# A selective-scan layer on one core: beta added by an accumulating DMA, and one more state's product on POOL

## The reference, cut to what matters

```
# selective scan: dt, Bm, Cm and z come from projections of x; 256 channels, 16 states per channel
h[n] = exp(A[n] * dt) * h[n] + dt * B[n] * x          # along time, for each state n
y    = sum over n of h[n] * C[n]  + D * x
y    = (y * silu(z)) @ w_out.T + b_out
pre  = y + residual
out  = (pre - mean) / sqrt(var + eps) * gamma + beta  # norm 3, with gamma and beta
x    = layernorm(residual + out)                      # norm 4: residual + beta + gamma * normed
# then the feed-forward layer starts with its own layernorm (norm 5), and norm 6 ends the model
```

## Time and profile before

| | |
|---|---|
| median of 3 runs | 1092.55 us (1088.25 to 1092.70) |
| the profiled execution's own time | 1091.53 us |
| its span, first to last instruction | 1089.7 us |
| mean granted clock of TensorE | 0.966 of full speed |
| DVE busy | 934.5 us (86% of the span) |
| POOL busy | 716.1 us (66%) |
| ACT busy | 847.9 us (78%) |
| PE busy | 977.5 us (90%), with modelled ends |

### The profile page before, as it was taken

The page is one execution under the profiler, slowest core; times in us unless marked ns, Lnnn a source line. Parts: engine busy times, 40 slices in busy tenths (PEclk is TensorE's granted clock), DMA queues, the critical chain, the costliest instruction groups (busy, mean ns, idle before and its releaser), DMA issues. The chain is left out here.

```text
span 1089.7 us, 17921 instructions
## 1 busy us (share of the span) xinstructions
PE 977.5 (90%) x5598; PEld 738.8 (68%) x5598; DVE 934.5 (86%) x1232; ACT 847.9 (78%) x1650; POOL 716.1 (66%) x603
## 2 busy tenths in 40 slices
PE   6999999999978999998657599999999989997987
PEld 4677777777754555555545487777777777786776
DVE  7999999999963897965799999999999999999851
ACT  7778878878746668767877889898998989897843
POOL 3456466766761111323779999998989989998630
PEclk9999999999998999999778799999999999999899
DMA  6443434433415002112987768477676757776401
GB/s 187 124 143 114 139 110 141 122 94 116 120 52 195 0 1 78 39 39 88 245 167 168 137 155 170 118 179 153 164 147 164 151 135 188 151 151 141 88 4 38
DMA packets 93921, 133.86 MB, mean 123 GB/s; under 512 B 8706, under 2 KB 48642, under 8 KB 93828
## 3 DMA queue, kind: packets, MB, share of 16 engines
q1 hardware_dynamic: 93828, 132.73, 49.1%
HBM read 116.45 MB, written 14.16 MB: 120 GB/s over the span
## 5 line engine op out<-in xcount | busy, mean ns | idle before, releaser
L2345 DVE TENSOR_TENSOR_SCAN oa<-bank_a,h,oa 128x512 f32<-128x512 f32 x128 | 159.7, 1269 | 12.7 <-ACT h L2020 9.8
L2345 DVE TENSOR_TENSOR_SCAN ob<-bank_a,h,ob 128x512 f32<-128x512 f32 x128 | 160.1, 1268 | 10.2 <-ACT bank_a L2011 6.1
L1820 PE MATMUL bank_m<-w,f_h 128*128 128x256 f32 x448 | 104.3, 383 | 0.0
L1491 POOL TENSOR_TENSOR oa<-ob,x1T 128x1024 f32<-128x1024 f32 x8 | 18.8, 2355 | 129.5 <-DVE ob L1391 129.5
L2011 ACT ACTIVATE bank_a<-s,A 128x512 f32<-128x512 f32 x128 | 86.8, 684 | 17.8 <-DVE ob L2345 8.9
L2011 ACT ACTIVATE bank_a<-dtc,A 128x512 f32<-128x512 f32 x128 | 86.9, 684 | 14.1 <-DVE ob L2345 6.9
L1765 PE MATMUL bank_y<-ident,ob 128*128 128x128 f32 x512 | 71.2, 285 | 26.1 <-POOL ob L2581 14.4
L1820 PEld LDWEIGHTS bank_m<-w,f_h 128*128 128x128 f32 x448 | 84.7, 192 | 14.2 <-issue 3.6
L1765 PEld LDWEIGHTS bank_y<-ident,ob 128*128 128x128 f32 x512 | 62.6, 147 | 36.6 <-POOL ob L2581 15.3
L883 POOL TENSOR_TENSOR xd<-xs,L 128x512 f32<-128x512 f32 x32 | 34.0, 1063 | 76.1 <-DVE xs L662 76.1
L1765 PE MATMUL bank_y<-ident,oa 128*128 128x128 f32 x512 | 70.9, 284 | 14.1 <-DVE oa L2351 14.0
(11 more groups left out here) (403 smaller groups left out, 2925.8 us busy)
## 6 DMA issues: line engine op xcount, KB each, us to landing
Bb<-CB_rows SPq DMA_DIRECT2D x128, 256.0 KB, 6.1
Cb<-CB_rows SPq DMA_DIRECT2D x128, 256.0 KB, 5.8
abc<-decays SPq DMA_DIRECT2D x32, 512.0 KB, 4.4
Ebc<-ramps SPq DMA_DIRECT2D x64, 128.0 KB, 3.1
uT<-in_uT SPq DMA_DIRECT2D x8, 512.0 KB, 4.2
u<-in_u SPq DMA_DIRECT2D x8, 512.0 KB, 3.9
x_tokens<-x2s SPq DMA_DIRECT2D x8, 512.0 KB, 3.5
x_rows<-x1T SPq DMA_DIRECT2D x8, 512.0 KB, 2.9
```

The lines of the kernel that those rows point to most:

```text
L1820: i = e.matmul(to, f_h[:, k, c * CH:(c + 1) * CH], w2[:, k, :], start=False, stop=(c % 2 == 1 and k == KF - 1))
L2345: e.tensor_tensor_scan(s[:, k, :], p_a[k][:, :], s[:, k, :], h0[:, n, k:k + 1], ALU.mult, ALU.add).then_inc(v_s, 1)
```

## The change

- `shifted` no longer computes: POOL issues a DMA that reads the row beta from DRAM, 1 KB for each of 4 token groups and each of 128 partitions (512 KB in all), and adds it to `x2` in SBUF. `summed` waits for this DMA instead of for POOL's sum. In the last block (`end_shifted`, L2661) the sum stays on POOL; only its count starts at 0.
- State 3 joins `on_pool`: its product leaves DVE, where it stood between the scans of states 4 and 5, and stands on POOL between `into(cur, 6)` and `into(cur, 7)`. ACT's `spread_C(cur, 3)` goes. All counts that are worked out from `on_pool` follow: SP's `load_C(7)` now waits for POOL's product of state 3, PE's `add_up(3)` too, and `into(7)` too.

```diff
+            beta_row = d["everywhere"].rearrange("(a o n) -> a o n", a=1, o=1)[:, :, sum(n for _, n in EVERYWHERE) - DM:]
-            p_g, on_pool = d_sem("p_g"), (0, 12, 14)
+            p_g, on_pool = d_sem("p_g"), (0, 3, 12, 14)
 # ACT
                         decay(cur, 4, 1)
-                        spread_C(cur, 3)
                         carry(cur, 3)
 # DVE
-                    e.wait_ge(p_xb, Z + p + 1)
+                    e.wait_ge(p_xb, p + 1)
                         scan(cur, 4, 1)
-                        product(cur, 3)
                         scan(cur, 5, 0)
 # POOL
                 def shifted(b):
                     e.wait_ge(v_pre, 2 * b + 2)
-                    e.sem_inc(step, 1)
-                    e.tensor_tensor(x2, x2, rowwise(bet), ALU.add).then_inc(p_xb, 1)
+                    e.dma_start(x2, beta_row.to_broadcast([P, NC, DM]), accum_op=ALU.add).then_inc(ld_beta, DMAS)
                 def summed(b):
                     e.wait_ge(p_gam, b + 1)
-                    e.wait_ge(p_xb, b + 1)
+                    e.wait_ge(ld_beta, DMAS * (b + 1))
                         into(cur, 6)
+                        product(cur, 3)
                         into(cur, 7)
```

More of the change, by code:

```diff
@@ L1563, in build @@
             p_b, p_l3, p_xb, p_gam, p_add, p_l4, p_l6 = (d_sem("p_" + n) for n in ("b", "l3", "xb", "gam", "add", "l4", "l6"))
-            ld_xT, ld_x2, st_o = (d_sem(n) for n in ("ld_xT", "ld_x2", "st_o"))
+            ld_xT, ld_x2, st_o, ld_beta = (d_sem(n) for n in ("ld_xT", "ld_x2", "st_o", "ld_beta"))
             pair, single = (p_m[0], p_m[2]), p_m[1]
```

## The result

The changed kernel takes 1097.55 us, the median of 15 runs (1091.74 to 1099.05); the kernel before took 1091.69 us on the same chip (15 runs, 1088.25 to 1094.96). Over all these runs the ratio of after to before is 1.0043, with a 95% interval of 1.003 to 1.0056: a loss of 4.7 us (3.3 to 6.1), small and clear of no change. The profiled execution took 1096.12 us with a span of 1094.3, against 1091.53 and 1089.7 before.

What follows compares the result with a forecast made beforehand. POOL's turn was to set the period: 2.63 - 2.47 + 1.7 = 1.86 us in each of 7 periods, 13.0 less 6.9 us of waits, +6.1 us on 1091.53, 1097.6, taken as 1098; range 1087 to 1110.

Steps and rivals of the forecast that it cites:

- The issue: POOL's time to issue the accumulating DMA in place of `shifted`: taken as 1.7 us, bounds 0.38 to 4.9 us.
- 7 x (0.16 + X) - 6.9: POOL's added time over 7 periods: product +2.63, sum -2.47, X for the DMA's issue, less 6.9 us of waits.
- the break-even: Issue time on POOL at which its longer turn just uses up its waits for statistics: 0.83 us.
- the 6.9 us of room: POOL's waits for DVE's statistics ahead of `norm45`, 5 places over all blocks, taken off the added time as one sum.
- Rival D: Nothing shows: POOL's issue between 0.8 and 1.6 us, loss under 5.4 us; chance 0.22.
- ACT's gain: ACT's copy of C for state 4 comes 0.35 us earlier each period, at most 2.8 us in 8 blocks.
- rival B: DVE sets the pace: the full 1.11 us comes out in each of 8 blocks, -8.9 us, 1083.6; chance 0.10.
- rival A: Light issue, 0.4 to 0.8 us: POOL keeps its room, ACT's 0.35 us sets the time, 1088 to 1092; chance 0.17.
- "nothing" for `add_up(3)`: PE's `add_up(3)` starts at 796.94, POOL's product is there at 795.4: no cost.
- The new wait: POOL's `summed` waits for the DMA's landing: 17 us of cover from six POOL instructions, against 7.2 for a load; no cost.
- SP's queue: B of state 9, issued behind C of state 7, lands at 801.9, wanted at 802.7: no cost, 0.8 us to spare.
- Rival C: DMA lands over 17 us after issue or delays state 9's B over 0.8 us; landing at 19 gives 1112; chance 0.09.

Runs made afterwards that it cites:

- the first and seventh experiment: Changed kernel with state 3's product back on DVE, DMA kept: 1.0013 of the kernel before; the same with POOL's sum in block 0's tail: 1.0016.

## Why the prediction was right, and where it was off

**The number.** Of the forecast 1098 us the measured median, 1097.55, is only 0.5 us off, and part of that is luck: the sum was +6.1 us and the loss by the ratio is 4.7. The issue was taken 1.9 us too dear in all, and the rest of the sum 0.5 us too cheap. The loss forecast as likeliest was one of over 0.5%; it was 0.43%.

**What sets the time.** POOL's turn does, as forecast: the instructions that POOL has to run one behind the other in a period. The runs, put beside the prediction's formula 7 x (0.16 + X) - 6.9 with X as POOL's timeline of each has it (to the start of the next instruction; without POOL's idle time behind it):

| kernel | X, us | formula | period by period | measured, us (95%) |
|---|---|---|---|---|
| no beta | 0 | none | 0.3 | 0.0 (-1.6 to 1.5) |
| plain DMA | 0.91 | 0.6 | 2.4 | 4.4 (2.7 to 5.9) |
| 4 KB pieces | 1.03 | 1.4 | 2.8 | 3.1 (1.5 to 4.5) |
| the change | 1.43 | 4.2 | 4.4 | 4.7 (3.3 to 6.1) |
| part of the sum, no DMA | 1.57 | 5.2 | 5.3 | 5.4 (3.5 to 7.2) |
| POOL's sum kept | 2.47 | 11.5 | 11.6 | 11.6 (9.5 to 13.7) |
| two DMAs | 2.57 | 12.2 | 12.3 | 12.0 (9.9 to 14.1) |

The measured column is ratio less one, times the median of before on the same chip. The waits of ACT for `norm45` grow roughly with X: 5.1 us without beta, 7.3 with the plain DMA, 7.6 in the changed kernel, 7.3 with part of the sum, 10.2 and 9.6 in the last two. From 1.4 us on the formula holds within 0.5 us. The plain DMA shows that it fails below; the 4 KB pieces lie 1.7 us above it, at the edge of their interval.

**The mis-sized term: the issue.** I took 1.7 us, from the power of 128x8 numbers; the row has 1.35 us and 1.43 to the next start. That is 7 x 0.27 = 1.9 us of my 6.1; the sum with the measured term is +4.2 against the measured +4.7. The Trainium skill (DMA: Bandwidth & Descriptors, Specifications and Anatomy of one DMA) has about 1 µs to the first byte of a DMA through GpSimd, and calls the generation of descriptors small. That isn't the same quantity, but the plain copy's 0.83 us of POOL's own time is near it, and the accumulating one's 1.35 us isn't small where POOL sets the pace.

**The step that was wrong in form: the break-even.** I pooled the 6.9 us of room over seven periods, and so had a break-even at an issue of 0.83 us. But the prediction itself reads that two of the seven have no room, and I now take it that room doesn't pass from one period to the next. Tail by tail, POOL waited in the kernel before 0, 0, 1.6, 1.6, 1.6, 0.8 and 1.2 us. A turn longer by G = 0.16 + X costs G less the period's room, and never less than zero; for the plain DMA that is 2 x 1.07 + 0.27 = 2.4 us, and for the change 2 x 1.59 + 0.79 + 0.39 = 4.4. The column "period by period" is this. It is worked out after the result and no run tests it alone, but the measured times of the two kernels in question lie nearer to it. The plain DMA still costs 2.0 us more than it gives; that is of the size of the 1.4 and 1.7 us that the DMA alone costs in the first and seventh experiment, and the kernel that would tell, the issue's 0.9 us of POOL's time without a DMA, was not run.

This count is not the whole of it either. The sum that went stood ahead of `norm36`, the product that came stands behind it. In the kernel without beta POOL takes 21.68 us from `norm36` to `norm45` (810.78 less 789.10) where it took 20.68 (809.49 less 788.81), although the 1.61 us of wait for the statistics are gone from it. So the product alone uses up the room ahead of `norm45`, whatever beta costs, and an issue can hide only in the wait for norm 3's statistics. The prediction read that wait (1.1 us) and left it out of its sum. In the kernel without beta it is 0, 0, 0.8, 1.4, 0.7, 0 and 0.2 us, tail by tail. Counted from there the plain DMA would cost 3.8 us, which fits, and the change 7.0 us, which is above its interval. Neither count fits every kernel.

One reading of a row was wrong without harm to the sum: the waits for rows of B are not mostly in block 0. Of the 8.4 us, 2.2 lie there and 6.2 in the later blocks; the changed kernel still has 5.2 of these.

Rival D, a small loss with an issue between 0.8 and 1.6 us, is in truth where the change landed: my own mechanism, at its lower end.

**ACT's gain.** The prediction's 0.35 us a period is there: from the scans of state 4 to the copy of C for that state's product it was 3.76 us before and is 3.32 now. By `stats4` 0.28 us of it are left in the changed kernel, and 0.46 us in the one without beta. ACT's timeline of the changed kernel, against the earlier trace rows, has the copy of C right behind the carry, without the 0.35 us of idle time:

```profile
795.37 0.69 ACT L2029 ACTIVATE xc<-bank_m,columns 128x512 f32<-128x512 f32 x1 [0.63 <-PE bank_m L40]
795.96 0.19 ACT L2022 ACTIVATE h<-oa 128x2 f32<-128x2 f32 x1
796.05 0.59 ACT L2018 ACTIVATE bank_c<-Cb 128x512 f32<-128x512 f32 x1
```

The 8.9 us of rival B are refuted by the kernel without beta: no issue holds POOL there, and the time is that of before. The prediction reckoned with up to 2.8 us of rival A in that case; the measured 0.0, with 1.6 us of gain as its bound, shows less. The rows show one place where they went. `norm36` waits for norm 3, which lies ahead of state 4, and from there to the next `drive` POOL has hardly a gap and one instruction more; this stretch is 33.26 us (822.36 less 789.10), and with it the period shrinks by only 0.18 us of the 0.46. No run has the product ahead of `norm36`, so this stays a reading of the rows. Another candidate is the rows of B.

**PE.** I had "nothing" for `add_up(3)`. The rows show 0.51 us: POOL's product ends at 798.46, and PE takes `add_up(3)` up at 799.66, since the matmuls of two other products (the first of them at 796.11) stand ahead of it in its own order.

```profile
793.35 1.98 PE L40 MATMUL bank_m<-s,w_xz 128*128 128x512 f32 x4 [1.43 <-ACT xc L2029]
...
797.93 1.89 PE L1822 MATMUL bank_m<-w,f_h 128*128 128x256 f32 x8
799.66 1.04 PE L1767 MATMUL bank_y<-ident,oa 128*128 128x128 f32 x8
```

From the x projection to `add_up(3)` it is 6.31 us, exactly as in the earlier trace rows. PE's order didn't move, and DVE, early now, reaches it too soon. I looked for a cost at POOL's product; it is in PE's program.

**The new wait and SP's queue.** `summed` never waited in the changed kernel's profile; it comes 18.3 us after the issue's start, and the landings take 9.4 to 12.4. Rival C happened once in the eight profiles with POOL's DMA, with the product on DVE: 18.0 us of landing and 3.0 us of wait in the first tail. "Nothing" for the load of state 9's B was too kind, as a statement on B's rows altogether: they land 1.2 us later in the median in the changed kernel, and 0.4 to 1.6 us later in all the others, with the product on POOL or POOL's DMA or both. I take the product's part, without a run that shows it, for the loads that SP issues in a bunch once POOL's product of state 3 frees their buffer.

**What stays open.** The early blocks: three kernels that left one or both alone gave 1.0032, 1.0032 and 0.9991, none of it clear of the kernel that it is to be compared with. The 1.4 and 1.7 us of the DMA alone, whose intervals begin at 1.0000 and 1.0001. And why the plain DMA, with an issue 0.5 us shorter, costs nearly as much as the change.

## What to carry to other kernels

Where engines are busy for 91 to 96% of a period, taking an instruction off the busiest of them is worth only what the next-late engine allows, here 0.46 us of 1.1, and nothing of it in the end; ask first which wait ends last behind it. Idle time on the engine that takes the work over was not one sum of room here: 6.9 us counted together promised that an issue of 0.8 us would be free, and one of 0.9 cost 4.4. Count it period by period, and ask on which side of a wait work is added and on which it is taken away. And an issue isn't free on an engine whose turn is closed: it is an instruction with a price, and most of the price is per DMA.

## What the runs showed of the hardware

- POOL issues a plain DMA of 512 pieces of 1 KB in 0.83 us, an accumulating one in 1.35, an accumulating one of 128 pieces of 4 KB in 0.95, and two accumulating ones of 256 pieces in 2.49 together. I had expected the pieces to make the price.
- The same 3.67 MB are 3696 packets in the software queue when 1 KB pieces are added, and 1008 when they are copied plainly, or added in 4 KB pieces.
- 512 KB from POOL land after 10.1 us in the median (accumulating), 10.2 (plain) and 8.9 (accumulating, 4 KB pieces), against 7.1 to 7.4 for SP's load of the same size in the same kernels. The addition isn't what makes it slow. That POOL issues it isn't shown to be the reason either: the two stand at different places of the period and read different data. One landing took 18.0 us.
